# Scores of two head groups made together over half the array's rows, in the slots that also carry expert work

## The chip, the cores and the metric

The kernel runs on one core of one Trainium2 chip. The metric is the device time of one execution in microseconds; smaller is better. Before the change, three runs gave 626.65, 628.77 and 629.81 us, a median of 628.77 us. The profile shows one further execution, of 622.62 us.

## The reference

Sixty-four sequences of 128 rows and 128 columns go through a cross-attention with 77 keys and 16 heads of depth 8, and then through a mixture of eight experts of which each row uses two. Both results are added to the input.

```python
x = x + tanh(g_xattn[0]) * xattn(layernorm(x), ctx, ctx, wq, wk, wv)
x = x + tanh(g_ffn[0])   * ffn(layernorm(x), Wr, br, W1, b1, W2, b2)

def xattn(q, k, v, wq, wk, wv):
    Q, K, V = split(q @ wq.T), split(k @ wk.T), split(v @ wv.T)
    scores = einsum('bhqd,bhkd->bhqk', Q, K) / sqrt(8)
    out = einsum('bhqk,bhkd->bhqd', softmax(scores), V)
    return out.transpose(0, 2, 1, 3).reshape(B, S, 128)

def ffn(x, Wr, br, W1, b1, W2, b2):
    logits = x @ Wr + br                       # 8 experts, the best two kept
    h = relu(einsum('btd,edh->bteh', x, W1) + b1)
    return einsum('bte,bteh,ehd->btd', gates, h, W2) + gates @ b2
```

## The kernel before

The program is written out engine by engine, with semaphores between the engines. Everything is ordered by *slots*. In slot `t` each engine issues its share of several sequences at different stages: the maxima of the scores of sequence `t - 8`, the scores, exponentials and values of sequence `t - 13`, and the normalising of sequence `t - 14`. Each engine issues in program order, so an instruction that waits holds all that stands behind it on its engine.

A sequence's 16 heads are worked on as four *head groups* `h` of four heads `j`. The stacked keys of a group (`k_st`) are laid over the 128 partitions so that head `j` has its numbers in the 32 partitions from `32 j` and zeros elsewhere. One score matmul of a head takes 128 partitions of keys (77 columns, the weights) and of queries (128 columns, streamed). `scores(b, h)` (L549) makes the four heads of a group into one of two PSUM banks, `score_bank[h % 2]`. `exp_scores(b, h)` (L864) on ScalarE turns that bank into `probs[h]` in one instruction. `values(b, h)` (L563) multiplies `probs[h]` with the values, 4 heads with 9 columns each into four different 32-partition strips of `oT_bank`; in float32 each takes two passes, so the profile counts 8.

From slot 43 on there is expert work between. Rows are sorted by expert into tiles of 128, and four tiles are a *quad*. A quad's slot (`QUAD_AT`: 43 to 50, 55 to 62, 67 to 73, 75, and later ones from 78) makes the hidden layer in two halves, `hidden_part(q, 0)` and `hidden_part(q, 1)` (L639 to L641), with `relu` (L930) on ScalarE after each; the slot after makes the output with `rows_out(q, 0)` and `rows_out(q, 1)` (L653, L655), which ScalarE copies out in `outputs(q)` (L939).

Of the quad slots, 24 (43 to 50, 55 to 62, 67 to 73 and 75) still carry attention. By `t % 4`, other steps for groups of four sequences come in:

- in slots with `t % 4 == 0` and `== 2`, TensorE transposes the maxima into `o_bank` (`turn_max`), ScalarE copies them out (`turned_max`, `nmT`, L852), and `turn_o` (L576) of TensorE waits for that copy before it writes `o_bank`;
- in slots with `t % 4 == 2`, `project_k` (L482) on TensorE and `k_high` (L870) on ScalarE, up to slot 62;
- in slots with `t % 4 == 3`, `turn_x2` (L511) on TensorE, and `rows_high` (L906) and `turned_x2` (L897) on ScalarE; slot 75 has `dense_rows_high` (L967) in place of `rows_high`, behind `turned_x2`.

On ScalarE the order of a quad slot is: `output_rows` (L858), exponential 0, `turned_max`, the steps of the groups, `relu(q, 0)`, exponential 1, `outputs(q - 1)`, exponential 2, then `k_high` or `rows_high` and `turned_x2`, exponential 3, `relu(q, 1)`.

Of the kernel before, what the change touches and what calls it, by code (L numbers as in the profile page):

```python
# [36 lines left out]
def flamingo_kernel(nc, x, ctx_t, g_xattn, g_ffn, w_att_t, w_router, b_router, w1, b1, w2, b2, out):  # L37
# [39 lines left out]
    t = 0  # L77
# [28 lines left out]
    with ExitStack() as stack:  # L106
# [192 lines left out]

        def ranks_before(s):  # L300
            return len([c for c in range(NC) if RANKED[c] < s])
# [27 lines left out]

        def early_scores(t):  # L330
            return False

        def values_behind(b, t):
            return active(b) and not early_scores(t + 1)
# [135 lines left out]
        def _(pe):  # L470
# [44 lines left out]
            def max_scores(b, h):  # L515
# [8 lines left out]
                if h == (3 if early_scores(b + MAX_LAG) else 2) and b % NB == 0 and g >= 3:  # L524
                    pe.wait_ge(s_logit, g - 2)
# [26 lines left out]

            def values(b, h):
# [25 lines left out]
            def route(g, t):  # L579
                if g == 0:  # L580
                    pe.wait_ge(s_bias, 16 * 3)
                pe.wait_ge(s_max, clip(HG * (t - MAX_LAG) + (3 if early_scores(t) else 1 if lent(t - MAX_LAG, 1) else 2), HG * B))
# [147 lines left out]
            def slot_of_quads(t):  # L730
                u, r = t // NB, t % NB
                mx, sc, ob = t - MAX_LAG, t - SCORE_LAG, t - OUT_LAG
                if active(sc):
                    scores(sc, 0)
                if active(mx):
                    max_scores(mx, 0)
                if active(sc):
                    scores(sc, 1)
                if active(ob):
                    values(ob, 3)  # L740
                older_maxima(t)
                first_group_step(t)
                if active(mx):
                    max_scores(mx, 1)
                for q in quads_at(t):
                    hidden_part(q, 0)
                if active(sc):
                    scores(sc, 2)
                if active(mx):
                    max_scores(mx, 2)  # L750
                if active(sc):
                    values(sc, 0)
                if active(ob):
                    turn_o(ob, t)
                if r == 0 and group_on(u - 5):
                    route(u - 5, t)
                for q in quads_at(t - 1):
                    rows_out(q, 0)
                if active(sc):
                    scores(sc, 3)  # L760
                    values(sc, 1)
                middle_group_step(t)
                for q in quads_at(t - 1):
                    rows_out(q, 1)
                if active(mx):
                    max_scores(mx, 3)
                if active(sc):
                    values(sc, 2)
                for q in quads_at(t):
                    hidden_part(q, 1)  # L770
                last_group_step(t)
                if values_behind(sc, t):
                    values(sc, 3)

            def slot(t):
# [4 lines left out]
                if early_scores(t):  # L780
                    slot_of_quads(t)
                    return
                if active(sc):
# [9 lines left out]
                if active(sc):  # L793
# [9 lines left out]
                if active(sc):  # L803
                    values(sc, 0)
                    scores(sc, 2)
# [5 lines left out]
                if active(sc):  # L811
                    values(sc, 1)
                    scores(sc, 3)
# [9 lines left out]
                if values_behind(sc, t):  # L823
# [16 lines left out]
        def _(act):  # L840
# [153 lines left out]
            def slot(t):  # L994
# [20 lines left out]
                if early_scores(t):  # L1015
                    if active(sc):
                        exp_scores(sc, 0)
                    for q in quads_at(t - 2):
                        store_y(q)
                    if active(ob):  # L1020
                        output_rows(ob)
                    if active(sc):
                        exp_scores(sc, 1)
                    older_maxima(t)
                    first_group_step(t)
                    for q in quads_at(t):
                        name_biases(q)
                        relu(q, 0)
                else:
                    if active(ob):  # L1030
                        output_rows(ob)
                    for q in quads_at(t - 2):
                        store_y(q)
                    for n in dense_at(t):
                        dense_relu(n)
                    if active(sc):
                        exp_scores(sc, 0)
# [604 lines left out]
```

## Time and profile before

| | |
|---|---|
| median of 3 runs | 628.77 us (626.65 to 629.81) |
| the profiled execution | 622.62 us |
| its span, first to last instruction | 620.9 us |
| TensorE busy | 548.5 us, 88% of the span |
| ScalarE busy | 355.8 us, 57% |
| the chain that ended last | 65% TensorE, 11% VectorE, 7% ScalarE |

The span is the time between the first and the last instruction that the profiler saw; the execution's own time has 1.7 us around it. A matmul row of the timeline gives its start and its length until its modelled end; matmuls of one stream overlap, so what one of them takes of the engine is the distance between starts. A row of several (x4) has the start of the first and the length until the end of the last. In brackets stands the time for which the engine was idle before the row, and what ended it. PE is TensorE's matmuls, ACT is ScalarE.

### The profile page before, as it was taken

To read this page: it belongs to the slowest core of one execution; us is meant where nothing else is said; L and a number is where in the kernel's file an instruction comes from. 1 tells how busy PE (TensorE), PEld (TensorE's weight loads), DVE (VectorE), ACT (ScalarE), POOL (GpSimd) and SP (SyncE) were. 2 spreads that over 40 slices of the span, in tenths; PEclk is the share of its full clock that TensorE was granted. 3 is DMA by queue.
4 is the path that set the end of the run, shared out by engine and by line. 5 is a ranking of instruction groups with operands and counts; after the bars stand their busy time and mean duration, and the time that the engine had idled before them with its cause. 6 is when DMAs were issued, how large, how long until landed. Compare 5 with 4: busy or idle time off the path is not lost.

```text
span 620.9 us, 18511 instructions
## 1 busy us (share of the span) xinstructions
PE 548.5 (88%) x6213; PEld 392.2 (63%) x6213; DVE 373.4 (60%) x1361; ACT 355.8 (57%) x834; POOL 273.0 (44%) x283
## 2 busy tenths in 40 slices
PE   3659899989998999999889999898898869999996
PEld 1325455555555567766567767656676559898885
DVE  5477688888977765436775556685654324224354
ACT  2117776765665566756665676665565645657431
POOL 6530001100575103545363534674545566677771
PEclk9959899999997999999989999999999969999999
DMA  4936655763753656553585644493432435686431
GB/s 133 170 101 175 144 104 147 169 114 120 184 154 98 143 69 167 120 130 114 107 151 126 143 107 136 114 171 87 100 101 82 90 98 150 153 157 165 117 101 52
DMA packets 158121, 78.65 MB, mean 127 GB/s; under 512 B 85088, under 2 KB 153312, under 8 KB 158032
## 3 DMA queue, kind: packets, MB, share of 16 engines
q1 hardware_dynamic: 119760, 45.65, 33.9%
q0 software_dynamic: 7168, 14.69, 9.9%
q10 hardware_dynamic: 31104, 17.13, 9.9%
q8 instruction: 54, 0.88, 0.6%
q14 instruction: 35, 0.29, 0.2%
HBM read 30.72 MB, written 36.75 MB: 109 GB/s over the span
## 4 chain that ended last, share of the span: by engine, by line
PE 65%; DVE 11%; issue 9%; ACT 7%; DMA 3%; POOL 3%; SPq 1%; ACTq 1%; DVEq 0%
PE y L655 12%; PE scores L549 8%; PE bank_oT L563 8%; PE o L576 4%; PE hidden_p L639 4%; ACT probs L864 3%; DVE neg_max L1177 3%; PE hidden_p L640 3%; PE max_scores L526 3%; PE max_scores L587 2%; PE o L696 2%; PE bank_oT L696 2%; PE hidden_p L641 2%; PE group L495 2%; POOL xs_dram L1531 2%
## 5 line engine op out<-in xcount | busy, mean ns | idle before, releaser
L864 ACT ACTIVATE probs<-scores 77x512 f32<-77x512 f32 x256 | 150.0, 598 | 40.5 <-PE scores L549 39.7
L1531 POOL DMA_INDIRECT xs_dram<-rows,at x112 | 110.3, 985 | 76.1 <-PE max_scores L526 38.3
L1177 DVE TENSOR_REDUCE neg_max<-max_scores 128x4 f32<-128x308 f32 x166 | 79.3, 478 | 94.9 <-PE max_scores L526 89.3
L1546 POOL DMA_INDIRECT back<-ys_dram,at x112 | 108.0, 964 | 64.3 <-PE max_scores L526 22.1
L563 PE MATMUL bank_oT<-probs,v_cols 77*9 77x128 f32 x2048 | 105.5, 279 | 14.3 <-ACT probs L864 13.5
L549 PE MATMUL scores<-q_st,k_st 128*77 128x128 bf16 x1024 | 106.7, 229 | 0.2
L549 PEld LDWEIGHTS scores<-q_st,k_st 128*77 128x77 bf16 x1024 | 71.7, 118 | 50.6 <-issue 44.5
L930 ACT ACTIVATE hidden<-hidden_p,b_cols 128x128 f32<-128x128 f32 x256 | 73.5, 373 | 38.0 <-PE hidden_p L641 30.4
L655 PE MATMUL y<-w_sb,hidden 128*128 x608 | 92.9, 291 | 0.0
L655 PEld LDWEIGHTS y<-w_sb,hidden 128*128 128x128 f32 x608 | 81.5, 195 | 2.3
L1492 POOL TENSOR_TENSOR rstd<-ve,power 128x4 f32<-128x4 f32 x16 | 17.7, 1106 | 122.0 <-DVE ve L1145 120.3
L563 PEld LDWEIGHTS bank_oT<-probs,v_cols 77*9 77x9 f32 x2048 | 30.4, 88 | 61.9 <-ACT probs L864 32.3
L939 ACT COPY ys<-y 128x512 f32<-128x512 f32 x38 | 22.3, 587 | 71.9 <-PE y L655 71.9
L639 PE MATMUL hidden_p<-xsT,w_sb 128*128 128x128 bf16 x256 | 53.6, 229 | 10.5 <-ACT hidden L930 6.1
L526 PE MATMUL max_scores<-k_st,q_st 128*128 128x308 bf16 x166 | 50.4, 303 | 4.3 <-issue 1.7
L641 PE MATMUL hidden_p<-xsT,w_sb 128*128 128x128 bf16 x256 | 53.0, 224 | 0.0
L640 PE MATMUL hidden_p<-xsT,w_lo 128*128 128x128 bf16 x256 | 52.8, 223 | 0.1
L576 PE MATMUL o<-ident,oT 128*128 128x128 f32 x256 | 39.8, 279 | 10.9 <-ACT oT L858 8.8
L1486 POOL TENSOR_TENSOR rstd<-ve,power 128x4 f32<-128x4 f32 x16 | 16.4, 1026 | 72.1 <-DVE ve L1118 56.2
L858 ACT COPY oT<-bank_oT 128x512 f32<-128x512 f32 x64 | 37.8, 591 | 17.0 <-PE bank_oT L563 16.7
L1177 DVE TENSOR_REDUCE neg_max<-hidden_p 128x4 f32<-128x308 f32 x78 | 36.9, 473 | 10.0 <-PE hidden_p L526 9.7
L639 PEld LDWEIGHTS hidden_p<-xsT,w_sb 128*128 x256 | 25.3, 99 | 26.1 <-issue 21.6
(163 smaller groups left out, 970.7 us busy)
## 6 DMA issues: line engine op xcount, KB each, us to landing
ys_dram<-ys ACTq DMA_DIRECT2D x38, 256.0 KB
q_st<-q_dram SPq DMA_DIRECT2D x16, 512.0 KB, 3.9
k_st<-k_dram SPq DMA_DIRECT2D x64, 77.0 KB, 4.2
xs_all<-x SPq DMA_DIRECT2D x16, 256.0 KB, 4.0
q_dram<-q_hl SPq DMA_DIRECT2D x16, 256.0 KB, 2.7
xs_dram<-zeros_b ACTq DMA_DIRECT2D x16, 256.0 KB, 2.8
out<-xs_all SPq DMA_DIRECT2D x16, 256.0 KB
k_dram<-k_hl SPq DMA_DIRECT2D x48, 77.0 KB
```

The costliest lines, as they stand in the source:

```text
L526: mm(max_to(b, h)[:, 0:PER * KEYS], q_st[g % 3][:, h, seq_cut(b, S)], k_st[g % 3][:, h, b % NB, :, :].rearrange("p j k -> p (j k)"), start ...
L549: last = mm(score_bank[h % 2][0:KEYS, j * S:(j + 1) * S], k_st[g % 3][:, h, b % NB, j, :], q_st[g % 3][:, h, seq_cut(b, S)], start=True, s ...
L563: last = mm(oT_bank[ROWS * j:ROWS * j + VW, h * S:(h + 1) * S], v_cols[g % 3][:, b % NB, h * PER + j, :], probs[h][:, j * S:(j + 1) * S], ...
L639: mm(o, w_hi[:, at_w], tiles[:, 0, cut], start=True, stop=False, skip_group_check=True)
L640: mm(o, w1_lo[:, at_w], tiles[:, 0, cut], start=False, stop=False, skip_group_check=True)
L641: last = mm(o, w_hi[:, at_w], tiles[:, 1, cut], start=False, stop=True, skip_group_check=True)
L655: last = mm(o, hidden[:, (2 * q + t // 2) % 4, t % 2, m, :], w2_sb[:, bass.ds(w + m * 128, 128)], start=False, stop=(m == HC - 1), skip_gr ...
L864: nc.scalar.activation(probs[h][:], score_bank[h % 2][0:KEYS, :], ACT.Exp, scale=SCALE).then_inc(s_exp, 1)
L930: last = nc.scalar.activation(hidden[:, k % 4, i, m, :], of[:, j * 128:(j + 1) * 128], ACT.Relu, bias=b1_cols[:, bass.ds(held[q][2 * half ...
L1177: V.tensor_reduce(neg_max[:, i // 2, :, h, i % 2], max_to(b, h)[:, 0:PER * KEYS].rearrange("p (j k) -> p j k", j=PER), AXIS_X, ALU.max, ne ...
L1531: G.indirect_dma_start(out=xs_dram[c % 2], out_offset=bass.IndirectOffsetOnAxis(ap=at[k][c % 4][:, i:i + 1], axis=0), in_=rows[c % 2][:, i ...
L1546: G.indirect_dma_start(out=back[k][:, b % 16, :], out_offset=None, in_=ys_dram[c % 2][0:TILES[c] * 128, :], in_offset=bass.IndirectOffsetO ...
```

## The change

In the 24 quad slots that carry attention (`paired(b)`), the scores of head groups 0 and 1 are made by one function, `score_pair(b, 0)`, at the place where `scores(b, 0)` stood, and those of groups 2 and 3 by `score_pair(b, 2)`, where `scores(b, 2)` stood. Each of the eight matmuls takes 64 partitions in place of 128. Heads 0 and 1 lie in the lower 64 partitions and heads 2 and 3 in the upper 64, and the matmuls alternate between the two halves. The lower half writes to `score_bank[0]`, the upper half to `score_bank[1]`; so a bank now holds two heads of either group, and `probs[first]` and `probs[first + 1]` are filled accordingly (`cut_of` says where a head is). `values(b, h)` takes heads from both, and so waits for both exponentials of its pair.

ScalarE issues exponential 1 right behind exponential 0, ahead of `turned_max`, the steps of the groups and `relu(q, 0)`; exponential 2 ahead of `outputs(q - 1)`; exponential 3 stays where it was. Functions that were behind `early_scores`, which returned False, are removed; they issued nothing. All other slots are as before.

```diff
+        def paired(b):
+            return bool(quads_at(b + SCORE_LAG))
+
+        def cut_of(b, h, j):
+            at = 2 * (h % 2) + j % 2 if paired(b) else j
+            return slice(at * S, (at + 1) * S)
...
+            def score_pair(b, first):
...
+                pe.wait_ge(s_exp, HG * b + first)
+                for h in (first, first + 1):
+                    for n in range(PER):
+                        part, j = n % 2, 2 * (n % 2) + n // 2
+                        rows_of = slice(2 * ROWS * part, 2 * ROWS * (part + 1))
+                        last = mm(score_bank[part][0:KEYS, cut_of(b, h, j)], k_st[g % 3][rows_of, h, b % NB, j, :],
+                                  q_st[g % 3][rows_of, h, seq_cut(b, S)], start=True, stop=True, skip_group_check=True)
+                        if h > first and n >= 2:
+                            last.then_inc(p_st, 1)
...
             def values(b, h):
...
-                pe.wait_ge(s_exp, HG * b + h + 1)
+                pe.wait_ge(s_exp, HG * b + (h // 2 * 2 + 2 if paired(b) else h + 1))
                 for j in range(PER):
+                    of = probs[h // 2 * 2 + j // 2 if paired(b) else h]
...
-                              probs[h][:, j * S:(j + 1) * S], start=True, stop=True, skip_group_check=True)
+                              of[:, cut_of(b, h, j)], start=True, stop=True, skip_group_check=True)
...
             def slot(t):
...
-                if active(sc):
+                pairs = active(sc) and paired(sc)
+                if pairs:
+                    score_pair(sc, 0)
+                elif active(sc):
                     scores(sc, 0)
...
-                if active(sc):
+                if active(sc) and not pairs:
                     scores(sc, 1)
...
                 if active(sc):
                     values(sc, 0)
+                if pairs:
+                    score_pair(sc, 2)
+                elif active(sc):
                     scores(sc, 2)
...
             def exp_scores(b, h):
                 act.wait_ge(p_st, HG * b + h + 1)
                 if b:
-                    act.wait_ge(p_pv, HG * (b - 1) + h + 1)
+                    act.wait_ge(p_pv, HG * (b - 1) + (h // 2 * 2 + 2 if paired(b - 1) else h + 1))
...
+                if active(sc):
+                    exp_scores(sc, 0)
+                if pairs:
+                    exp_scores(sc, 1)
+                older_maxima(t)
+                first_group_step(t)
+                for q in quads_at(t):
+                    name_biases(q)
+                    relu(q, 0)
+                if active(sc) and not pairs:
+                    exp_scores(sc, 1)
+                if pairs:
+                    exp_scores(sc, 2)
                 for q in quads_at(t - 1):
                     outputs(q)
-                if active(sc):
+                if active(sc) and not pairs:
                     exp_scores(sc, 2)
```

How instructions move is shown for slots 46 and 47. On ScalarE at the start of slot 46 (`t % 4 == 2`), before the change; `nmT` is the copy for which `turn_o` waits, `hidden` the first half's relu:

```order
L858 COPY oT<-bank_oT 128x512
L948 DMA ys_dram0<-ys1 128x4x128
L864 ACTIVATE probs0<-scores0 77x512
L852 COPY nmT<-o 64x128
L917 TENSOR_LOAD tile_b0
L930 ISA
L930 ACTIVATE hidden<-hidden_p,b1_cols 128x128
```

The same place with the change:

```order
L835 COPY oT<-bank_oT 128x512
L925 DMA ys_dram0<-ys1 128x4x128
L841 ACTIVATE probs0<-scores0 77x512
L841 ACTIVATE probs1<-scores1 77x512
L829 COPY nmT<-o 64x128
L894 TENSOR_LOAD tile_b0
L907 ISA
L907 ACTIVATE hidden<-hidden_p,b1_cols 128x128
```

Exponential 1 now stands ahead of the copy of the maxima and of the relu.

On ScalarE in the later part of slot 47 (`t % 4 == 3`), from behind `relu(q, 0)`, before; `ys` is `outputs(q - 1)`, `rows` and `xT2` are `rows_high` and `turned_x2`:

```order
L864 ACTIVATE probs1<-scores1 77x512
L939 COPY ys1<-y 128x512
L864 ACTIVATE probs2<-scores0 77x512
L906 CAST rows0<-xn2 128x4x128
L897 COPY xT2<-group 128x512
L864 ACTIVATE probs3<-scores1 77x512
L930 ISA
```

The same place with the change:

```order
L841 ACTIVATE probs2<-scores0 77x512
L916 COPY ys1<-y 128x512
L883 CAST rows0<-xn2 128x4x128
L874 COPY xT2<-group 128x512
L841 ACTIVATE probs3<-scores1 77x512
L907 ISA
```

Exponential 2 went ahead of the copy of the outputs; exponential 3 has the same three instructions between it and the expert output as before, less one exponential.

On TensorE in slot 47, from `turn_x2` (`group<-ident,xn2`) to the second half of the hidden layer, before, with the semaphores that each waits for:

```order
L511 MATMUL group<-ident,xn2 128x128 [waits xn2_made,v_made,k_lo_made]
L511 MATMUL group<-ident,xn2 128x128 x3
L563 MATMUL bank_oT<-probs1,v_cols2 9x128 [waits exp_made]
L563 MATMUL bank_oT<-probs1,v_cols2 9x128 x3
L549 MATMUL scores1<-q_st2,k_st2 77x128 [waits exp_made]
L549 MATMUL scores1<-q_st2,k_st2 77x128 x3
L526 MATMUL max_scores<-k_st0,q_st0 128x308 [waits max_made]
L563 MATMUL bank_oT<-probs2,v_cols2 9x128 [waits exp_made]
L563 MATMUL bank_oT<-probs2,v_cols2 9x128 x3
L639 ISA [waits hidden_made]
```

The same place with the change:

```order
L512 MATMUL group<-ident,xn2 128x128 [waits xn2_made,v_made,k_lo_made]
L512 MATMUL group<-ident,xn2 128x128 x3
L581 MATMUL bank_oT<-probs0,v_cols2 9x128 [waits exp_made]
L581 MATMUL bank_oT<-probs0,v_cols2 9x128
L581 MATMUL bank_oT<-probs1,v_cols2 9x128 x2
L527 MATMUL max_scores<-k_st0,q_st0 128x308 [waits max_made]
L581 MATMUL bank_oT<-probs2,v_cols2 9x128 [waits exp_made]
L581 MATMUL bank_oT<-probs2,v_cols2 9x128
L581 MATMUL bank_oT<-probs3,v_cols2 9x128 x2
L657 ISA [waits hidden_made]
```

The scores of group 3 are gone from between the values of groups 1 and 2, and the values of group 2 now read `probs3` too, so their wait is for exponential 3.

## Rows read from the trace of the kernel before

**Rows 1.** The page: its head, TensorE's busy time (share, instructions), the chain by engine.

```profile
span 620.9 us, 18511 instructions
PE 548.5 (88%) x6213; PEld 392.2 (63%) x6213; DVE 373.4 (60%) x1361; ACT 355.8 (57%) x834; POOL 273.0 (44%) x283
...
PE 65%; DVE 11%; issue 9%; ACT 7%; DMA 3%; POOL 3%; SPq 1%; ACTq 1%; DVEq 0%
```

**Rows 2.** Busy time by stretch, slots 43 to 51; granted clock is the third number from the end.

```profile
215.20:295.90 80.70, 76.41 (x920) 56.73 (x920) 43.98 (x164) 51.78 (x135) 28.53 (x29) 1.00 0.52 119
```

**Rows 3.** Timeline of TensorE, slot 48: start, length, engine, line, what, [idle before].

```profile
261.33 0.38 PE L549 MATMUL scores<-q_st,k_st 128*77 128x128 bf16 x4
261.55 0.29 PE L526 MATMUL max_scores<-k_st,q_st 128*128 128x308 bf16 x1
261.69 0.60 PE L576 MATMUL o<-ident,oT 128*128 128x128 f32 x4
...
264.54 0.41 PE L563 MATMUL bank_oT<-probs,v_cols 77*9 77x128 f32 x8
264.88 0.42 PE L549 MATMUL scores<-q_st,k_st 128*77 128x128 bf16 x4
265.13 0.29 PE L526 MATMUL max_scores<-k_st,q_st 128*128 128x308 bf16 x1
...
267.71 0.41 PE L563 MATMUL bank_oT<-probs,v_cols 77*9 77x128 f32 x8 [0.35 <-ACT probs L864]
```

**Rows 4.** Timeline of ScalarE, slot 48: the copy of the outputs, exponentials 2 and 3.

```profile
266.58 0.59 ACT L939 COPY ys<-y 128x512 f32<-128x512 f32 x1 [3.34 <-PE y L655]
267.06 1.08 ACT L864 ACTIVATE probs<-scores 77x512 f32<-77x512 f32 x2
```

**Rows 5.** Waits of TensorE, slots 43 to 51: total us, times, longest.

```profile
PE bank_oT L563 <- ACT probs L864: 2.5, 5, 1.1
PE hidden_p L639 <- DVE neg_max L1177: 0.7, 1, 0.7
```

**Rows 6.** Timeline of both engines, slot 46 (the remainder of division by four is 2).

```profile
243.03 0.27 ACT L852 COPY nmT<-o 64x128 bf16<-64x128 bf16 x1
...
243.46 0.60 PE L576 MATMUL o<-ident,oT 128*128 128x128 f32 x4
...
247.14 0.59 ACT L939 COPY ys<-y 128x512 f32<-128x512 f32 x1 [2.09 <-PE y L655]
...
248.11 0.41 ACT L870 CAST k_hl<-group 128x308 bf16<-128x308 f32 x1
...
248.37 0.41 PE L563 MATMUL bank_oT<-probs,v_cols 77*9 77x128 f32 x8
248.41 0.61 ACT L864 ACTIVATE probs<-scores 77x512 f32<-77x512 f32 x1
...
249.48 0.41 PE L563 MATMUL bank_oT<-probs,v_cols 77*9 77x128 f32 x8
```

**Rows 7.** Timeline of TensorE, slot 47 (remainder 3): values of groups 2 and 3.

```profile
257.41 0.41 PE L563 MATMUL bank_oT<-probs,v_cols 77*9 77x128 f32 x8
...
258.88 0.41 PE L563 MATMUL bank_oT<-probs,v_cols 77*9 77x128 f32 x8
```

**Rows 8.** Timeline of ScalarE, slot 47: outputs, rows_high, turned_x2, exponential 3.

```profile
256.27 0.59 ACT L939 COPY ys<-y 128x512 f32<-128x512 f32 x1 [2.13 <-PE y L655]
...
257.24 0.61 ACT L906 CAST rows<-xn 128x512 bf16<-128x512 f32 x1
257.75 0.59 ACT L897 COPY xT<-group 128x512 f32<-128x512 f32 x1
258.22 0.61 ACT L864 ACTIVATE probs<-scores 77x512 f32<-77x512 f32 x1
```

**Rows 9.** Timeline of both engines, slot 43, first of its run of quads: values of group 2, exponential 3.

```profile
219.72 0.41 PE L563 MATMUL bank_oT<-probs,v_cols 77*9 77x128 f32 x8
219.92 0.60 ACT L864 ACTIVATE probs<-scores 77x512 f32<-77x512 f32 x1
```

More of the change, by code:

```diff
@@ L328, in two_banks @@
             return QUAD_AT[q] >= GATED_ALL
[L330 to L334, printed above, removed]
         def dense_at(s):
@@ L523, in max_scores @@
                     pe.wait_ge(s_relu, 2 * quads_before(b + MAX_LAG))
-                if h == (3 if early_scores(b + MAX_LAG) else 2) and b % NB == 0 and g >= 3:
+                if h == 2 and b % NB == 0 and g >= 3:
                     pe.wait_ge(s_logit, g - 2)
@@ L551, in scores @@
                 last.then_inc(p_st, 1)
+            def score_pair(b, first):
+                g = b // NB
+                if b % NB == 0 and first == 0:
+                    pe.wait_ge(s_nst[0][g % 3], 16 * (g // 3 + 1))
+                if b % NB == 2 and first == 0:
+                    pe.wait_ge(s_nst[1][g % 3], 16 * (g // 3 + 1))
+                pe.wait_ge(s_exp, HG * b + first)
[7 more added lines that the diff above has]
+                            last.then_inc(p_st, 1)
             def values(b, h):
@@ L581, in route @@
                     pe.wait_ge(s_bias, 16 * 3)
-                pe.wait_ge(s_max, clip(HG * (t - MAX_LAG) + (3 if early_scores(t) else 1 if lent(t - MAX_LAG, 1) else 2), HG * B))
+                pe.wait_ge(s_max, clip(HG * (t - MAX_LAG) + (1 if lent(t - MAX_LAG, 1) else 2), HG * B))
                 if g:
@@ L728, in last_group_step @@
                         ranks(c)
-            def slot_of_quads(t):
-                u, r = t // NB, t % NB
-                mx, sc, ob = t - MAX_LAG, t - SCORE_LAG, t - OUT_LAG
-                if active(sc):
-                    scores(sc, 0)
-                if active(mx):
-                    max_scores(mx, 0)
-                if active(sc):
[L738 to L746, printed above, removed]
-                if active(sc):
[L748 to L773, printed above, removed]
             def slot(t):
@@ L779, in slot @@
                     name_weights(q)
[L780 to L783, printed above, removed]
+                pairs = active(sc) and paired(sc)
+                if pairs:
+                    score_pair(sc, 0)
+                elif active(sc):
                     scores(sc, 0)
@@ L822, in slot @@
                 last_group_step(t)
-                if values_behind(sc, t):
+                if active(sc):
                     values(sc, 3)
@@ L1014, in slot @@
                     b2_part(t - 16)
[L1015 to L1037, printed above, removed]
-                    older_maxima(t)
-                    first_group_step(t)
-                    for q in quads_at(t):
-                        name_biases(q)
-                        relu(q, 0)
-                    if active(sc):
-                        exp_scores(sc, 1)
+                if active(ob):
+                    output_rows(ob)
+                for q in quads_at(t - 2):
+                    store_y(q)
+                for n in dense_at(t):
+                    dense_relu(n)
+                pairs = active(sc) and paired(sc)
+                if active(sc):
+                    exp_scores(sc, 0)
[10 more added lines that the diff above has]
+                    exp_scores(sc, 2)
                 for q in quads_at(t - 1):
                     outputs(q)
-                if active(sc):
+                if active(sc) and not pairs:
                     exp_scores(sc, 2)
@@ L1410, in slot @@
                     q_low(u - 1)
-                if early_scores(t) and active(mx):
-                    head_max(mx, 2)
                 if r == 0 and group_on(u - 5):
@@ L1417, in slot @@
                     heads_normed(ob)
-                if not early_scores(t) and active(mx):
+                if active(mx):
                     head_max(mx, 2)
```

1 line of the change is left out of this document (removed).

## Prediction

> **What bounds the kernel now.** I read the page first: TensorE is busy for 88% of the span and makes 65% of the chain that ended last [rows 1]. Then the stretches: in slots 43 to 51 it is busy for 76.41 of 80.70 us at the full granted clock, 1.00, which is 2.4 GHz [rows 2]. Over these slots TensorE waits little, but where it waits it is mostly the values that wait for an exponential, 2.5 us in five waits [rows 5]. So a quad slot is a row of TensorE work, with one place at which ScalarE sets the time. The timeline shows that place. In slot 48 the values of group 2 start at 267.71 after 0.35 us of waiting [rows 3], and ScalarE has copied the expert output at 266.58 and begun exponential 2 at 267.06 [rows 4]. The chain there is: last output matmul, copy, exponential, values. From one ScalarE start to the next it takes 0.48 us, from the exponential's start to the values 267.71 - 267.06 = 0.65 us.
>
> **What a pair block costs.** Four score matmuls take 261.55 - 261.33 = 0.22 us, 0.055 each; behind values they take 265.13 - 264.88 = 0.25, so 0.03 more where the first weights can't be loaded ahead [rows 3]. Today's four groups of a slot thus take 0.25 + 0.22 + 0.25 + 0.25 = 0.97 us.
>
> No row has matmuls of 64 partitions. The nearest are the values, which also use parts of the array: eight passes take 264.88 - 264.54 = 0.34 us [rows 3]. The four transposes beside them are float32 passes of the same 128 columns; four of them reach 0.60 us with the last one's 0.27 or so in it, 0.11 apart [rows 3]. Eight in a row would be 0.88, so the four strips do run side by side, as two waves of 0.11, and 0.12 us is left over, in which nothing is streamed. I read that as the array emptying before it is used in another shape. Between values and scores both sides pay it already. A pair block is a third shape: at its start it replaces scores that came behind values, so nothing is added; at its end maxima follow, where today no such gap is, and 0.12 is added.
>
> From below: halves side by side, no gap, 4 x 0.055 = 0.22 us. From above: no overlap, 8 x 0.055 + 0.03 + 0.12 = 0.59. Between: side by side with the gap, 0.22 + 0.03 + 0.12 = 0.37; if the eight weight loads come one after another at 0.03 each, 0.39. I take 0.39, since the values rows, the nearest, show both overlap and gap. Two blocks are then 0.78 against 0.97: TensorE has only 0.19 us less work in a slot.
>
> The Trainium skill says, in "TensorE: Matmul & The Clock Gate", section "LDWEIGHTS (loading the stationary operand)", that a weight load takes its columns divided by 1.2 in nanoseconds, however few the rows; that is an estimate of 64 ns for 77 columns and 0.66 us for a block. The trace disagrees: load and matmul together pass at 0.055 us [rows 3].
>
> **What the waits do.** The saving is spread: 0.25 + 0.22 + 0.25 = 0.72 us of scores stood ahead of the expert outputs and 0.25 behind them. After the change all 0.78 stands ahead. So the copy of the outputs comes 0.06 us later, and the 0.25 saved behind it lies where TensorE waits for ScalarE anyway. Before, the values of group 2 needed exponential 2; now they need exponential 3, the next thing on ScalarE behind the copy where nothing else is queued, so at the same distance. Slots by their remainder (`t % 4`):
>
> - Remainders 0 and 1, twelve slots: about +0.07 each. Two of remainder 1 (slots 69 and 73) have no group step between the maxima and the hidden layer and so are held there by the relu of the quad before; such a wait, 0.7 us, is in [rows 5] under a name of VectorE whose work was long done. It hides the longer first block, and they come to -0.08 (-0.22 for group 1's scores, +0.14 for the second block). Remainder 0 adds up to 0.2 in three slots, where `turn_o` waits for `nmT`, as below. Together about +0.9.
> - Remainder 2, five slots. Exponential 1 now goes ahead of `nmT`; one exponential lasts 0.49 from start to start (1.08 less the 0.59 of one, [rows 4]). `nmT` moves from 243.03 to 243.52, ends 0.27 later, and 0.06 after that (the 0.65 above less 0.59) `turn_o` can start, at 243.85 in place of 243.46: +0.39 [rows 6]. Behind it are the expert outputs, all in order. The second block adds 0.14. The copy of outputs moves to 247.14 + 0.53 = 247.67; then `k_high` 0.48 later, exponential 3 another 248.41 - 248.11 = 0.30 later, at 248.45, and the values of group 2 at 249.10 instead of 248.37: +0.73. Four slots have `k_high`; slot 70 has a later `nmT` against `turn_o` and no `k_high`, +0.14. Together 4 x 0.73 + 0.14 = +3.1.
> - Remainder 3 with outputs of a quad before (47, 59, 71). Ahead of exponential 3 stand `rows_high` and `turned_x2`. These slots are held by the relu at their start, so the copy moves by -0.08 to 256.19. `rows_high` follows 0.48 later, `turned_x2` 0.51 (257.75 - 257.24), exponential 3 0.47 (258.22 - 257.75), at 257.65 [rows 8]; the values of group 2 come at 258.30 instead of 257.41 [rows 7]. Group 3's values waited for exponential 3 before; free of waits they follow 249.48 - 248.37 = 1.11 later [rows 6], at 259.41 instead of 258.88: +0.53. Together +1.6.
> - First quads of a run (43, 55, 67, 75): no outputs to copy, but the same two steps ahead of exponential 3. Exponential 2 begins about where it did, because it needs the second block, so exponential 3 stays at 219.92 and group 2's values go from 219.72 to 219.92 + 0.65 = 220.57: +0.85 [rows 9], four times, +3.4.
>
> Sum: 0.9 + 3.1 + 1.6 + 3.4 = 9.0 us on the profiled execution's 622.62. That execution lies 6.15 us below the median of the runs, 628.77, with the same program; I add the sum to the median: 637.8 us.
>
> Two exponentials in a row cost ScalarE itself nothing: it has free time in all these slots, 57% busy overall [rows 1]. The relu of the first half comes 0.5 us later, hidden by the expert outputs that TensorE does before it needs that bank again. SP's stores of the maxima and of the queries start up to 0.5 us later, and their readers stand several slots on.
>
> **Rivals.**
> First, the halves don't overlap: a block is 0.59, 0.20 more. Remainder 2 hides the first block behind `nmT` and remainder 3 behind the relu, so it comes to some 0.3 a slot over 24 slots, +7.2: 645 us. Against it is that the values' strips overlap; for it, that strips are columns and these are rows.
>
> Second, and not slower: the lost time is given back. TensorE also waits outside the paired slots; of the 2.5 and 0.7 us of [rows 5] four waits of 0.35 lie in paired slots, so 1.1 of the values' waits does not. If such waits end by something that does not shift with TensorE (a transfer, VectorE behind with older work), lateness is absorbed there. Three stretches with about 2 us each of such waits in and between them would return 6: 628.77 + 9.0 - 6 = 631.8. The point from which it decides is 5.9 us returned, where the rest is inside 0.5%. Against it: the releasers named are ScalarE's steps, and those start from TensorE's own results.
>
> Third, faster: a block costs half of today's scores and ScalarE is never waited for. Then 16 matmuls take the time of 8, 8 x 0.055 = 0.44 less in 24 slots, 10.6 us: 618.2. Both the gap in [rows 3] and the wait in [rows 4] speak against it.
> The Trainium skill speaks for that third one: "TensorEngine Tiling (Array Packing)", section "Theoretical Speedup", gives up to twice the rate where 64 partitions or fewer are summed.
>
> **How the numbers follow.** The likeliest case 0.71, 637.8 us; its own range 634 to 641, from a block at 0.22 (about 4.5 less, as `nmT` and the relu hold part of it) to one at 0.45 (some 2 more). No overlap 0.13, given back 0.11, faster 0.05. The range for the time takes in the first rival and the second down to a little more than 6 us returned: 630.5 to 645. A change under 0.5%, 3.1 us, can't be told from none. Slower by more: 0.71 + 0.13 = 0.84, less 0.01 for a likeliest case at its low end; same 0.11 + 0.01; faster 0.05.
>
> **What would show it.** Starts of the score matmuls in pairs less than 0.02 us apart, and about 0.39 us from a block's first to the maxima behind it, show the block. In slots 46, 50, 58 and 62 `turn_o` should wait about 0.4 us for `nmT`. In slots of remainder 3, and in 46 to 62 of remainder 2, values of group 2 should wait for exponential 3, by 0.8 to 1.2 us in remainder 3; that wait's total over TensorE should grow by several us. I am wrong if these waits don't grow, or if they do and the span doesn't.

## The result, and the profile after

The changed kernel takes 642.34 us (median of four runs, 634.71 to 645.33) against 627.71 us of the kernel before (four runs, 625.46 to 629.81): 1.024 times as long, with a 95% interval of 1.016 to 1.032. The forecast was 637.8 us. The profiled execution is the longest of the four, 645.33 us, and 22.7 us over the profiled execution of before. Its page, to be held against [rows 1]:

```profile
span 643.6 us, 18499 instructions
PE 555.2 (86%) x6201; PEld 393.4 (61%) x6213; DVE 374.6 (58%) x1361; ACT 357.0 (55%) x834; POOL 272.3 (42%) x283
...
PE 65%; DVE 11%; issue 9%; ACT 7%; DMA 3%; POOL 2%; ACTq 1%; SPq 1%; another core or an unknown queue 1%; DVEq 0%
```

TensorE is no less busy than before; its busy share fell because the span grew. A *block* is here one call of `score_pair`, eight matmuls. The second block of slot 47 in the timeline of TensorE (start, length, line, what):

```profile
255.69 0.41 PE L581 MATMUL bank_oT<-probs,v_cols 77*9 77x128 f32 x8
256.03 0.42 PE L565 MATMUL scores<-q_st,k_st 64*77 64x128 bf16 x8
256.38 0.30 PE L527 MATMUL max_scores<-k_st,q_st 128*128 128x308 bf16 x1
```

The eight matmuls take 0.42 us until the end of the last, whose own length is 0.22. So from the first start to the eighth it is 0.20 us; one after the other, at 0.055 each, it would be 0.39. In the trace's records of this block the two of a pair start 3 to 4 ns apart; of all pairs at full clock four in five start 2 to 4 ns apart, the others up to 33 ns. From the block's first start to the maxima it is 0.35 us.

The rest of slot 47 on TensorE, which answers to [rows 7]:

```profile
251.51 0.42 PE L565 MATMUL scores<-q_st,k_st 64*77 64x128 bf16 x8
...
258.17 0.41 PE L581 MATMUL bank_oT<-probs,v_cols 77*9 77x128 f32 x8
258.51 0.30 PE L527 MATMUL max_scores<-k_st,q_st 128*128 128x308 bf16 x1
259.97 0.41 PE L581 MATMUL bank_oT<-probs,v_cols 77*9 77x128 f32 x8 [1.16 <-ACT probs L841]
261.18 0.41 PE L581 MATMUL bank_oT<-probs,v_cols 77*9 77x128 f32 x8
261.52 0.42 PE L565 MATMUL scores<-q_st,k_st 64*77 64x128 bf16 x8
```

And on ScalarE, which answers to [rows 8]:

```profile
256.48 0.59 ACT L841 ACTIVATE probs<-scores 77x512 f32<-77x512 f32 x1 [1.12 <-PE scores L565]
257.84 0.58 ACT L916 COPY ys<-y 128x512 f32<-128x512 f32 x1 [0.77 <-PE y L673]
258.32 0.62 ACT L883 CAST rows<-xn 128x512 bf16<-128x512 f32 x1
258.84 0.59 ACT L874 COPY xT<-group 128x512 f32<-128x512 f32 x1
259.32 0.60 ACT L841 ACTIVATE probs<-scores 77x512 f32<-77x512 f32 x1
```

Exponential 2 is done before the outputs are; then come the copy of the outputs, two steps of the group, and only then exponential 3, for which TensorE waits 1.16 us. In slot 48, which has no such steps, exponential 3 stands right behind the copy of the outputs, and the values of group 2 still wait for it, answering to [rows 3] and [rows 4]:

```profile
269.05 0.58 ACT L916 COPY ys<-y 128x512 f32<-128x512 f32 x1 [0.77 <-PE y L673]
269.53 0.59 ACT L841 ACTIVATE probs<-scores 77x512 f32<-77x512 f32 x1
...
270.17 0.41 PE L581 MATMUL bank_oT<-probs,v_cols 77*9 77x128 f32 x8 [0.59 <-ACT probs L841]
```

Slot 46 on ScalarE, answering to [rows 6]:

```profile
243.30 1.10 ACT L841 ACTIVATE probs<-scores 77x512 f32<-77x512 f32 x2
244.27 0.27 ACT L829 COPY nmT<-o 64x128 bf16<-64x128 bf16 x1
...
248.46 0.59 ACT L916 COPY ys<-y 128x512 f32<-128x512 f32 x1 [0.77 <-PE y L673]
248.98 0.41 ACT L847 CAST k_hl<-group 128x308 bf16<-128x308 f32 x1
249.29 0.59 ACT L841 ACTIVATE probs<-scores 77x512 f32<-77x512 f32 x1
```

And on TensorE there:

```profile
242.37 0.42 PE L565 MATMUL scores<-q_st,k_st 64*77 64x128 bf16 x8
...
244.64 0.63 PE L594 MATMUL o<-ident,oT 128*128 128x128 f32 x4 [0.45 <-issue]
...
249.94 0.41 PE L581 MATMUL bank_oT<-probs,v_cols 77*9 77x128 f32 x8 [0.42 <-ACT probs L841]
251.17 0.41 PE L581 MATMUL bank_oT<-probs,v_cols 77*9 77x128 f32 x8
```

`turn_o` waits 0.45 us and starts 0.10 us behind the end of the copy `nmT`. The profile names no releaser here; in slot 50, where the wait is 0.61 us, it names `nmT`. Over the whole execution TensorE's values waited for exponentials as follows, before the change and after (total us, times, longest):

```profile
PE bank_oT L563 <- ACT probs L864: 13.5, 37, 1.1
```

```profile
PE bank_oT L581 <- ACT probs L841: 25.8, 45, 1.5
```

A slot's length is the distance between its first score matmul and the next slot's. Of the 24 paired slots 21 ran at full granted clock in both profiles. Forecast and measured, in us more than before:

| slots | forecast | measured |
|---|---|---|
| remainder 0: 44, 48, 60, 72 | 0.7 | 0.8 |
| remainder 1: 45, 49, 57, 61, 69, 73 | 0.1 | -0.7 |
| remainder 2: 46, 50, 58, 62, 70 | 3.1 | 3.8 |
| remainder 3: 47, 59, 71 | 1.6 | 1.7 |
| first of a run: 43, 67, 75 | 2.5 | 3.5 |
| these 21 | 8.0 | 9.1 |

Two of these sums agree with the forecast better than their slots do. In remainder 0 slot 44 became 0.3 us shorter, and 48, 60 and 72 became 0.2 to 0.4 longer. In the first quads, 0.8 us of slot 67 did not come back when the same kernel ran again (e7).

Of the other 13.6 us of the two profiled executions' difference, 13.4 lie where the granted clock was lower: slots 52 and 53 (+4.3), 55 and 56 (+5.1), 68 (+0.3), and behind slot 75 (+3.7), where 17 us passed at 1.2 GHz against 10 before. Busy time by stretch (the third number from the end is the granted clock): slot 51 after, slot 52 after, and then slot 52 before.

```profile
291.10:299.33 8.23, 6.69 (x85) 4.85 (x81) 4.62 (x17) 5.01 (x12) 4.07 (x5) 1.00 0.34 94
299.33:307.87 8.54, 8.54 (x73) 5.91 (x69) 5.13 (x19) 3.48 (x7) 0.13 (x1) 0.54 0.12 36
```

```profile
295.90:301.31 5.41, 5.20 (x73) 3.61 (x69) 3.98 (x14) 3.47 (x7) 0.05 (x1) 1.00 0.19 58
```

Slot 52 is not a paired slot and issues the same 73 matmuls. At a clock of 0.54 it takes 8.54 us instead of 5.41.

### The profile page after: what moved, and what is told of

Its sections match the earlier page's. It is cut to its first block, busy times and chain, and to the rows that moved or that the text cites. A ratio compares the mean times of both kernels' runs of the same rounds, so it can differ in the third digit from the quotient of the medians.

```text
span 643.6 us, 18499 instructions
## 1 busy us (share of the span) xinstructions
PE 555.2 (86%) x6201; PEld 393.4 (61%) x6213; DVE 374.6 (58%) x1361; ACT 357.0 (55%) x834; POOL 272.3 (42%) x283
## 4 chain that ended last, share of the span: by engine, by line
PE 65%; DVE 11%; issue 9%; ACT 7%; DMA 3%; POOL 2%; ACTq 1%; SPq 1%; another core or an unknown queue 1%; DVEq 0%
PE y L673 13%; PE bank_oT L581 8%; PE o L594 4%; PE scores L550 4%; PE hidden_p L657 4%; ACT probs L841 4%; PE hidden_p L658 3%; PE max_scores L527 3%; DVE neg_max L1144 3%; PE max_scores L605 3%; PE scores L565 3%; PE hidden_p L659 2%; PE o L714 2%; PE bank_oT L714 2%; PE group L496 2%
## 5 line engine op out<-in xcount | busy, mean ns | idle before, releaser
L841 ACT ACTIVATE probs<-scores 77x512 f32<-77x512 f32 x256 | 148.5, 597 | 78.0 <-PE scores L550 40.7
L673 PE MATMUL y<-w_sb,hidden 128*128 x608 | 96.5, 299 | 0.0
L673 PEld LDWEIGHTS y<-w_sb,hidden 128*128 128x128 f32 x608 | 84.6, 201 | 2.5
L550 PEld LDWEIGHTS scores<-q_st,k_st 128*77 128x77 bf16 x640 | 46.9, 122 | 35.6 <-issue 28.9
L550 PE MATMUL scores<-q_st,k_st 128*77 128x128 bf16 x640 | 68.5, 234 | 0.0
L657 PE MATMUL hidden_p<-xsT,w_sb 128*128 128x128 bf16 x256 | 54.6, 232 | 9.6 <-ACT hidden L907 6.6
L527 PE MATMUL max_scores<-k_st,q_st 128*128 128x308 bf16 x166 | 52.0, 313 | 5.9 <-DVE neg_max L1144 3.6
L659 PE MATMUL hidden_p<-xsT,w_sb 128*128 128x128 bf16 x256 | 54.2, 227 | 0.0
L594 PE MATMUL o<-ident,oT 128*128 128x128 f32 x256 | 41.4, 286 | 13.6 <-ACT oT L835 9.1
L1144 DVE TENSOR_REDUCE neg_max<-hidden_p 128x4 f32<-128x308 f32 x78 | 36.9, 473 | 11.7 <-PE hidden_p L527 11.1
L594 PEld LDWEIGHTS o<-ident,oT 128*128 128x128 f32 x256 | 30.2, 146 | 19.6 <-ACT oT L835 11.4
```

The source lines that it names most:

```text
L527: mm(max_to(b, h)[:, 0:PER * KEYS], q_st[g % 3][:, h, seq_cut(b, S)], k_st[g % 3][:, h, b % NB, :, :].rearrange("p j k -> p (j k)"), start ...
L550: last = mm(score_bank[h % 2][0:KEYS, j * S:(j + 1) * S], k_st[g % 3][:, h, b % NB, j, :], q_st[g % 3][:, h, seq_cut(b, S)], start=True, s ...
L594: last = nc.tensor.transpose(o_bank[:, h * S:(h + 1) * S], oT[:, h * S:(h + 1) * S], ident[:])
L657: mm(o, w_hi[:, at_w], tiles[:, 0, cut], start=True, stop=False, skip_group_check=True)
L673: last = mm(o, hidden[:, (2 * q + t // 2) % 4, t % 2, m, :], w2_sb[:, bass.ds(w + m * 128, 128)], start=False, stop=(m == HC - 1), skip_gr ...
L841: nc.scalar.activation(probs[h][:], score_bank[h % 2][0:KEYS, :], ACT.Exp, scale=SCALE).then_inc(s_exp, 1)
```

## Experiments

Two theories stood at the start. By the first the loss is late exponentials: values wait for the second exponential of a pair, and on ScalarE other work stands ahead of it. By the second the half-row blocks themselves cost the time. The lower clock came in as a third question. The forecasts of e1 to e5 are meant at an equal granted clock, so each is answered by the lengths of slots that ran at full clock, and the whole time is given beside it.

**e1_max_copy_first**: the copy of the maxima ahead of exponential 1.

```diff
+                older_maxima(t)
                 if pairs:
                     exp_scores(sc, 1)
-                older_maxima(t)
                 first_group_step(t)
```

> The changed kernel with one edit on ScalarE: in the paired slots the copy of the maxima (nmT) goes ahead of exponential 1 again. Late-exponentials theory: the waits of turn_o, 0.42 to 0.61 us in slots 46, 50, 58 and 62, go, and those slots fall from 9.15 to 9.43 us to about 8.7 to 8.9; slots 48 and 60 lose 0.1 to 0.2; in all 2.0 to 2.5 us less than the changed kernel at the same granted clock. The values' waits for exponentials stay at about 25.8 us. Rival, that the half-row blocks and their change of shape cost the time: the four slots keep their length within 0.1 us, the time only moves to another wait.

634.50 us (four runs). Slots 46, 50, 58 and 62 take 8.68, 8.95, 8.73 and 8.66 us instead of 9.15, 9.43, 9.19 and 9.15: 1.9 us, as expected, and slots 48 and 60 lost nothing. The waits for exponentials are 26.2 us. The wait of `turn_o` and its price are shown. The whole time fell by 7 to 8 us, more than the 2.0 to 2.5 expected: the mean granted clock of these four runs is 0.957, against 0.946 of the changed kernel's runs.

**e2_exp3_before_steps**: exponential 3 right behind the copy of the outputs.

```diff
+                if pairs:
+                    exp_scores(sc, 3)
                 if r == 2 and later_group(u):
                     k_high(u)
...
-                if active(sc):
+                if active(sc) and not pairs:
                     exp_scores(sc, 3)
```

> The changed kernel with one edit on ScalarE: in the paired slots exponential 3 goes right behind the copy of the expert outputs, ahead of k_high, rows_high, turned_x2 and dense_rows_high. Late-exponentials theory: slots 47, 59, 71 fall from 9.87 to 10.01 us to about 9.0 (the wait of 1.16 us to about 0.2), first-quad slots 43, 55, 67, 75 lose 0.9 to 1.3 each, slots 46, 50, 58, 62 0.3 each; the values' waits for exponentials fall from 25.8 to about 18 us; in all 7 to 8.5 us less than the changed kernel at the same granted clock. Rival, block costs: less than 2 us.

624.91 us (ten runs), 1.001 (0.995 to 1.006) of the kernel before. Slots 47, 59, 71 take 9.08, 9.00, 8.91; slots 43 and 75 become shorter by 1.00 and 1.24, slots 46, 50, 58, 62 by 0.35 to 0.39. In the 20 paired slots at full clock in both profiles it is 8.2 us less than the changed kernel, as expected, and 0.5 more than the kernel before. The waits:

```profile
PE bank_oT L581 <- ACT probs L841: 17.8, 42, 1.1
```

The order of three ScalarE instructions in eleven slots is worth nearly the whole loss: 8.2 us at full clock, and the mean clock is back at 0.960. The theory of late exponentials holds.

**e3_whole_rows**: no half rows, all else as changed.

```diff
...
-                    for n in range(PER):
-                        part, j = n % 2, 2 * (n % 2) + n // 2
...
+                    for j in range(PER):
+                        last = mm(score_bank[h % 2][0:KEYS, cut_of(b, h, j)], k_st[g % 3][:, h, b % NB, j, :],
+                                  q_st[g % 3][:, h, seq_cut(b, S)], start=True, stop=True, skip_group_check=True)
+                    last.then_inc(p_st, 1)
...
```

> The changed kernel with the pairs of 64 rows undone and all else kept: score_pair issues the eight matmuls of a pair one after the other over 128 rows, each group into its own bank as in the kernel before; places, waits and ScalarE's order are the changed kernel's. Late-exponentials theory: halves run side by side and save 0.12 us a block (0.35 as the changed kernel's profile shows, against 8 x 0.055 + 0.03 = 0.47); with what turn_o's and the relu's waits hide about 4 us more than the changed kernel at the same granted clock, so some 13 us over the kernel before. Rival, that half-row blocks are what costs: 5 us or more less than the changed kernel. The 0.6 us waits at the values of group 2 stay.

637.19 us (four runs). As a whole time this is 4 to 5 us less than the changed kernel, where some 4 more were expected at an equal clock, and by itself it looks like what the second theory forecast. But the mean clock differs, 0.956 against 0.946. In the 18 slots at full clock in both, slot 67 left out, it takes 0.12 us a slot more than the changed kernel, some 2.9 us over 24 slots. So half rows are a small gain at an equal clock and the second theory falls; by the medians, the changed kernel's lower clock cost more than they gained.

**e4_wait_alone**: the kernel before, with the changed kernel's wait alone.

```diff
...
-                pe.wait_ge(s_exp, HG * b + h + 1)
+                pe.wait_ge(s_exp, HG * b + (h // 2 * 2 + 2 if paired(b) else h + 1))
```

> The kernel before with one edit on TensorE: in the 24 paired slots the values of groups 0 and 2 wait for the exponential of the group after theirs as well (1 and 3), as the changed kernel's do; scores, places and ScalarE's order stay as before. Late-exponentials theory: values of group 2 come 0.49 us later in slots of remainder 0 and 1, 0.69 in 46, 50, 58, 62, the slots 47, 59, 71 lengthen by 1.1, first-quad slots by 0.85: 12 x 0.49 + 0.49 + 4 x 0.69 + 3 x 1.1 + 4 x 0.85 = 16 us over the kernel before at the same clock. Rival, block costs and moves: under 3 us. On the clock: if longer gaps in TensorE's work bring the lower granted clock about, there should be more stretches at 1.2 GHz than in the kernel before here too, and more time on top.

649.84 us (four runs), 26.8 over the kernel before: no pair is made, and it loses more than the changed kernel. In the profile slots 43 to 75 are 24.3 us longer, not 16; 20.0 of it lie in the 21 paired slots at full clock in both. I had left out that the values of group 0 now wait for exponential 1, which in this order stands behind `relu(q, 0)`. In slots 43, 55, 67 and 75, with no expert outputs ahead of them, they wait 0.95 to 1.23 us; slot 43 grew by 2.0 us. The waits:

```profile
PE bank_oT L566 <- ACT probs L867: 33.7, 50, 1.4
```

In the changed kernel exponential 1 stands behind exponential 0, and in its slot 43 the values of group 0 wait for nothing.

**e5_exp3_before_outputs** and **e6_whole_rows_exp3_first**: the edit of e1, and exponential 3 behind exponential 2, ahead of the outputs; e6 has whole rows besides, as e3.

```diff
...
                 if pairs:
                     exp_scores(sc, 2)
+                    exp_scores(sc, 3)
                 for q in quads_at(t - 1):
                     outputs(q)
...
```

> The changed kernel with two edits on ScalarE in the paired slots: the copy of the maxima ahead of exponential 1, and exponential 3 right behind exponential 2, both ahead of the copy of the expert outputs. Late-exponentials theory: both need only the second block of scores, which is made before the expert outputs, so the values of group 2 wait for nothing; of the changed kernel's waits for exponentials 0.59 to 0.83 go in the twelve slots of remainder 0 and 1 (7.6 in all), 0.45 to 0.61 and 0.42 in slots 46, 50, 58, 62 (3.7), 0.59 in slot 70, 1.16 in 47, 59, 71 (3.5), 0.9 to 1.5 in 43, 55, 67, 75 (4.5): some 19 us less than the changed kernel, which stands 9.9 over the kernel before in the slots that run at 2.4 GHz in both; so about 9 us under the kernel before, 1.5%. Rival, block costs: no more than 5 us under the changed kernel. Third possibility, a wait at the copy of the outputs or at the relu takes over: slots of remainder 0 and 1 then lose less than 0.3 each.

> As e5_exp3_before_outputs, but the blocks take 128 rows, one matmul after the other, each group into its own bank. With no waits left to hide it, the whole rows' block should cost its 0.12 us in full, twice a slot in 24 slots: 5 to 6 us more than e5_exp3_before_outputs, so 3 to 4 us under the kernel before. If half rows were no gain once ScalarE is out of the way, the two would agree within 1.5 us.

e5: 606.89 us (six runs), 0.978 (0.974 to 0.982) of the kernel before, faster than both. e6: 613.62 us (eight runs), 0.988 (0.984 to 0.992). Slot 48 of e5 on ScalarE, answering to [rows 4], and on TensorE:

```profile
256.06 1.07 ACT L841 ACTIVATE probs<-scores 77x512 f32<-77x512 f32 x2 [2.08 <-PE scores L565]
257.42 0.58 ACT L916 COPY ys<-y 128x512 f32<-128x512 f32 x1 [0.28 <-PE y L673]
```

```profile
257.31 0.41 PE L581 MATMUL bank_oT<-probs,v_cols 77*9 77x128 f32 x8
257.65 0.30 PE L527 MATMUL max_scores<-k_st,q_st 128*128 128x308 bf16 x1
257.88 0.41 PE L581 MATMUL bank_oT<-probs,v_cols 77*9 77x128 f32 x8
```

Both exponentials end at 257.13, before the outputs are even made; ScalarE still waits 0.28 us for those, so the copy is not late, and TensorE goes through the values of group 2 without a wait. Waits for exponentials are 9.2 us in all. I expected 9 us under the kernel before and measured 16; in the 22 slots at full clock in both profiles it is 14.0. Slots of remainder 0 and 1 become 0.6 to 1.6 shorter against the changed kernel rather than 0.6 to 0.8.

Between e5 and e6 I expected 0.12 us twice a slot, 5 to 6 us. Slot 49 of both on TensorE, e5 and then e6:

```profile
259.33 0.42 PE L565 MATMUL scores<-q_st,k_st 64*77 64x128 bf16 x8
...
261.88 0.60 PE L594 MATMUL o<-ident,oT 128*128 128x128 f32 x4
...
263.86 0.42 PE L565 MATMUL scores<-q_st,k_st 64*77 64x128 bf16 x8
264.21 0.30 PE L527 MATMUL max_scores<-k_st,q_st 128*128 128x308 bf16 x1
```

```profile
260.80 0.64 PE L562 MATMUL scores<-q_st,k_st 128*77 128x128 bf16 x8
...
263.35 0.60 PE L590 MATMUL o<-ident,oT 128*128 128x128 f32 x4
...
265.33 0.64 PE L562 MATMUL scores<-q_st,k_st 128*77 128x128 bf16 x8
265.81 0.29 PE L526 MATMUL max_scores<-k_st,q_st 128*128 128x308 bf16 x1
```

A block of whole rows takes 0.48 us to the maxima, one of half rows 0.35. But `turn_o` starts 2.55 us into the slot in both: what the first block gains is lost again by the end of the hidden layer's first half, and what holds that half is not shown. Only the second block's gain stays, so the slots at full clock differ by some 0.1 us, 2 to 3 us in all. The medians are 6.7 us apart and the means of the runs 5.0; the mean clocks are 0.964 and 0.961, which single runs' scatter does not tell apart.

**e7_changed_again**: the changed kernel once more, beside the kernel before.

> The changed kernel as it is, beside runs of the kernel before on this chip. By the late-exponentials theory it stands 9 to 11 us over the kernel before at a like granted clock; the rest of the 14.6 us of the first comparison should go where the mean clocks are alike. If the changed kernel itself brings the lower clock about, its mean clock is again 0.01 below that of the kernel before and the difference is 14 us again.

641.62 us (four runs) against 623.07 (ten): 1.030 (1.022 to 1.037), a difference of 18.6 us where 14 were expected if the lower clock came back. Its slots repeat those of the first profile within 0.3 us wherever both are at full clock, but for slot 67: 7.13 instead of 8.08, which had 0.82 us of waiting that the profile lays to nothing. The mean granted clock was 0.945, and 0.947 in the first four runs; the ten runs of the kernel before beside it have 0.9625. So the lower clock belongs to the changed kernel. Slot 52 ran at the lower one here too, and in no other kernel's profile.

**e8_filled_waits** and **e9_whole_rows_again**: what lowers the clock? e8 adds matmuls whose result nobody reads; e9 is e3 again.

```diff
+                if pairs:
+                    q = quads_at(t)[0]
+                    pe.wait_ge(s_relu, 2 * q + 1)
+                    for _ in range(5 if r == 3 else 2):
+                        mm(hidden_bank[:], upper(w1_sb[:])[:, 0:128], xsT[q % 3][:, 0, :], start=True, stop=True,
+                           skip_group_check=True)
                 if active(sc):
                     values(sc, 2)
```

> The changed kernel, and in each paired slot TensorE makes matmuls ahead of the values of group 2 whose result nobody reads: two of 512 columns, five in slots of remainder 3 (0.21 us each at 2.4 GHz), into the hidden bank before the second half of the hidden layer overwrites it. They fill most of the waits of 0.59 and 1.16 us and add nothing to the path beyond 0.2 us a slot of remainder 3. If TensorE's emptiness in these waits brings the lower granted clock about, the mean clock rises from 0.946 to that of the kernel before (0.96) and the time falls by 4 to 7 us below the changed kernel's 642. If the falls of the clock have another cause, the mean clock stays at 0.943 to 0.950 and the time stays or rises by up to 3 us.

> The same kernel as e3_whole_rows, for its mean clock, which was 0.956 in four runs, against 0.946 in the eight of the changed kernel: the same waits, but 128 rows of the array at work in a block in place of two halves at once. If half rows are part of why the clock is lower, it stays near 0.956; if four runs were too few to tell, it comes out near 0.947. Time about 636 us in the first case, 640 in the second.

e8: 635.06 us (six runs, 624.57 to 637.82), mean clock 0.960. More work in the same slots took 6.6 us off the 641.62 of e7 (636.71 to 647.16), within the 4 to 7 expected. Slot 47 of e8 on TensorE:

```profile
251.81 0.30 PE L527 MATMUL max_scores<-k_st,q_st 128*128 128x308 bf16 x1
252.17 1.03 PE L797 MATMUL hidden_p<-xsT,w_sb 128*128 128x512 bf16 x4
253.27 0.41 PE L581 MATMUL bank_oT<-probs,v_cols 77*9 77x128 f32 x8
```

The stretch that was a wait of 1.16 us is filled (the records have four of the five), and the slot has its 10.01 us as before. In its profile, which is of the fastest of the six runs (624.57 us, clock 0.978), slots 52 and 53 run at full clock, 5.41 and 5.46 us. e9: 637.70 us (six runs), mean clock 0.955, as e3 with 0.956.

| kernel | runs | median us | kernel before beside it | mean clock |
|---|---|---|---|---|
| before | 33 | | 623.04, 623.07, 623.27 | 0.961 |
| changed (first and e7) | 8 | 642.34, 641.62 | 627.71, 623.07 | 0.946 |
| e1 | 4 | 634.50 | 623.04 | 0.957 |
| e2 | 10 | 624.91 | 623.04 | 0.960 |
| e3, e9 | 10 | 637.19, 637.70 | 623.04, 623.27 | 0.955 |
| e4 | 4 | 649.84 | 623.04 | 0.954 |
| e5 | 6 | 606.89 | 623.07 | 0.964 |
| e6 | 8 | 613.62 | 623.07 | 0.961 |
| e8 | 6 | 635.06 | 623.27 | 0.960 |

Single runs of one kernel scatter by 0.007 to 0.010 in this clock (standard deviation). Over the 33 runs of the kernel before, those at 0.950 or under have spans of 624 to 629 us and those at 0.970 or over 613 to 619, about 4 us for 0.01. The 0.015 between the changed kernel and before are thus worth some 6 us.

A straight line through these 33 runs (time against clock) gives what the kernel before would take at another run's clock. The changed kernel lies 11.3 us above it in the mean of its eight runs, e1 7.7, e2 1.5, whole rows (e3 and e9) 12.7, e4 23.6 and e8 9.8; e5 lies 15.0 below it and e6 11.7. Compared in this way half rows are worth 1.4 us in the changed kernel and 3.3 in e5.

What lowers the clock is shown in part. Filling the waits before the values of group 2 gives it back, 0.960 in six runs against 0.946 in eight, so emptiness in TensorE's work is a part of it. But the total of the waits does not decide: e1 waits as long for exponentials as the changed kernel (26.2 us) and has 0.957 in four runs, and e4 waits longer (33.7 us) and has 0.954. Whole rows with the same waits have 0.955, so how much of the array works may be another part, though the scatter of the runs leaves that unsure. Which wait brings on which fall was not settled: the falls come in stretches such as slot 52, whose own work and waits are as before.

## Why the prediction was right, and where it was not

**The block.** I took 0.39 us between 0.22 and 0.59; it is 0.35. Halves run side by side; the weight loads of the two halves don't stand in line, as they would at 0.39. The emptying that I read out of [rows 3] is there: from the last score's start to the maxima 0.15 us, of which 0.055 stream. The first rival, no overlap, with 0.59 us a block, is ruled out by the timeline and by e3 and e6, where whole rows take 0.48.

**No gain for the slots without group steps.** The copy of the outputs, then an exponential, then the values: as said, the chain is as long as before, and the saved 0.25 us became waiting. The waits in remainder 0 and 1 are 0.59 us where the 0.35 of [rows 3] and those 0.25 make 0.60 (0.83 in slots 72 and 73, where it was 0.48). Remainder 1 still came out 0.8 us below the forecast. In slots 45, 57 and 69 the values of group 0 come 0.23 to 0.36 us earlier in the slot than before, so the longer first block was hidden in 45 and 57 as well; in 49, 61 and 73 they come 0.08 to 0.17 earlier, and 73, for which the forecast had it hidden, did not become shorter.

**Remainder 2.** `turn_o` was to start 2.26 us into slot 46 and started at 2.27 (244.64 - 242.37); the values of group 2 were to come at 7.51 and came at 7.57. The slot grew by 0.90, not 0.73, because of what I left as it was behind them: values of group 2 to those of group 3 took 1.11 us in [rows 6] and takes 1.23 now. Between the two stands the second half of the hidden layer. Behind a wait it took that much longer in the kernel before as well: in slot 48, behind the wait of 0.35, it was 1.24. Why is not shown, and the wait is not the only thing that does it: in slot 43 of e2 and e5 it took 1.22 with no wait before it.

**Remainder 3.** Values of group 2 at 8.46 us into the slot, as forecast to the hundredth; the slot +0.56 against +0.53. Here e2 shows cause and price.

**First quads.** +0.98 and +0.91 for 43 and 75 against +0.85.

**The step that failed.** "I add the sum to the median": this took TensorE's granted clock to be the same on both sides. The sum itself, 9.0 us, is borne out: 8.0 was forecast and 9.1 measured in 21 slots, 0.8 of which is the wait in slot 67 that did not come back. At an equal clock the changed kernel lies 11.3 us over the kernel before, by the line above. What is missing of the 14.6 us, and of the 18.6 of e7, is for the most part the clock, 0.946 against 0.961, some 6 us, for which there was no term and no rival. The range held the time because it reached to the first rival, so for another reason than the one that came: that the time lies in the range is partly luck, that the slots agree is not.

**The other rivals.** Nothing was given back: slots 51, 54, 63 to 66 and 74 have the same lengths as before within 0.02 us when the clock is full. The faster case is what e5 makes of half its conditions: the values of group 2 wait for nothing in most paired slots, but a block still takes 0.35 us and not half of the scores' time. There the change of order alone (e6) brings 1.2% and the half rows a further 1.0%, clock included.

## What to carry to other kernels

When two results are made together and each consumer needs both, every consumer waits for the later one: look at what stands ahead of that one on its engine, by each kind of slot, before counting what the joint production saves. Here eleven slots with one or two copies in the wrong place cost some 8 us at full clock, more than 48 blocks of half rows returned (some 3 us), and with the exponentials moved ahead of the copies the same blocks are in the fastest version. A sum over slots holds at one clock only: here the kernel with the new waits ran at a lower mean clock and paid some 6 us for it, partly in slots that the change did not touch. So compare versions at an equal clock as well as by their times; by the times alone e3 would have spoken for the wrong theory.

## What the runs showed of the hardware

Two matmuls of 64 rows in the two halves of the array run at once, weight loads included. In the block shown they start 3 to 4 ns apart, and eight take 0.20 us from first to last start; eight over 128 rows take 0.48 us to the maxima behind them where these take 0.35. Going over to another shape of the array cost about 0.09 us in which nothing streamed (0.15 us from the block's last start to the maxima, 0.055 of it streaming). The first weights cost 0.03: in the trace's records the block's second pair starts 0.086 us behind the first, the later ones 0.056 apart.

Matmuls whose result nobody reads, put in where TensorE waited, made the kernel faster, 635.06 against 641.62 and 642.34 us, at a mean granted clock of 0.960 against 0.946. In the changed kernel's profile the clock fell to 0.54 in slot 52, though from slot 43 until then no wait of TensorE was longer than 1.16 us. The second half of the hidden layer, with the values behind it, took 1.21 to 1.25 us behind a wait in slots 44, 46 to 48 and 50 of the changed kernel, and 1.11 us without one in the same slots of e5.
